# Reordering the first tiles and tile 21 of a fused convolution and quantized feed-forward kernel

## What is computed

```python
out  = conv(x, weight, K=9, groups=4) + einsum('nd,od->no', c, c_weight)[:, :, None] + bias[None, :, None]
fake_quant(t, axis): s = max(max(|t|) / 127, 1e-8); q = clip(round(t / s), -128, 127) * s
qlinear(x, w) = einsum('bsh,oh->bso', fake_quant(x, -1), fake_quant(w, 1))
h    = silu(qlinear(out, w_gate)) * qlinear(out, w_up)      # 1376 wide
x    = x + qlinear(h, w_down)                               # back to 512
```

## Time and profile before

| what | value |
|---|---|
| median of 3 runs | 294.35 us (294.17 to 295.05) |
| profiled execution, its time | 294.47 us |
| profiled execution, its span | 292.9 us |
| busy: TensorE, weight loads | 281.7 us (96%), 164.4 us (56%) |
| busy: VectorE, ScalarE, GpSimd | 251.0, 194.3, 202.0 us (86%, 66%, 69%) |
| granted TensorE clock | full in all 40 slices |
| scale_gate (L803), all forms | 628 ns mean, 96 times |
| multiply_up (L813), all forms | 691 ns mean, 96 times |
| reduction of token_scales (L819) | 1576 ns mean, 32 times |
| scale_silu (L525), all forms | 1163 ns mean, 96 times |
| silu (L635), all forms | 674 ns mean, 96 times |
| round_h (L640), convert_h (L648), all forms | 1414 and 1309 ns mean, 32 times each |
| add_residual (L533) | 1273 ns mean, 24 times |

### The profile page before, as it was taken

How to read it: one execution, slowest core, us unless ns; L and a number is a source line. 1 busy time by engine, 2 the same in 40 slices (tenths; PEclk the granted TensorE clock), 3 DMA queues, 4 the chain that set the end, 5 groups by cost and what they waited for, 6 DMA issues and landing times.

```text
span 292.9 us, 4778 instructions
## 1 busy us (share of the span) xinstructions
PE 281.7 (96%) x1621; PEld 164.4 (56%) x1621; DVE 251.0 (86%) x405; ACT 194.3 (66%) x232; POOL 202.0 (69%) x213
## 2 busy tenths in 40 slices
PE   7998999999999999999999999999989999999995
PEld 7897656655455555554444556665434444444443
DVE  3879879999998988989888878897978889888885
ACT  2258999996686666564888845455688866666640
POOL 1595899998776766663788835556578887666623
PEclk9999999999999999999999999999999999999999
DMA  7999963579846877755489996524256684433355
GB/s 261 416 408 357 410 133 72 113 166 273 214 144 160 203 168 165 208 149 119 128 214 299 239 241 195 166 49 124 73 157 157 159 177 114 87 86 85 100 99 202
DMA packets 83847, 53.36 MB, mean 182 GB/s; under 512 B 69904, under 2 KB 70672, under 8 KB 83696
## 3 DMA queue, kind: packets, MB, share of 16 engines
q1 hardware_dynamic: 83536, 52.89, 67.3%
q10 hardware_dynamic: 288, 0.18, 0.3%
HBM read 27.75 MB, written 8.39 MB: 123 GB/s over the span
## 4 chain that ended last, share of the span: by engine, by line
PE 64%; DVE 9%; POOL 9%; DMA 7%; ACT 5%; issue 4%; SPq 1%; DVEq 0%; POOLq 0%
PE bank L1047 38%; PE bank L1067 19%; PE bank L931 7%; POOL sg_mem L525 4%; DMA xq_mem<-yq_mem 3%; DMA slab<-x_windows 3%; DVE h_mem L813 2%; DVE h_max L819 2%; POOL xq_mem L499 1%; DVE y_part L745 1%; DMA hq_mem<-hq_mem 1%; DVE sg_mem L803 1%; DVE gu_max L704 1%; POOL y_mem L499 1%; ACT sg_mem L635 1%
## 5 line engine op out<-in xcount | busy, mean ns | idle before, releaser
L1047 PE MATMUL bank<-wgu_t,xq_mem 128*128 128x512 bf16 (+1 forms) x768 | 155.9, 357 | 3.1 <-DVE h_mem L813 2.0
L525 POOL TENSOR_TENSOR sg_mem<-sg_mem,gu_scale_row 128x512 f32<-128x512 f32 (+1 forms) x96 | 111.4, 1163 | 64.3 <-ACT sg_mem L635 64.0
L1047 PEld LDWEIGHTS bank<-wgu_t,xq_mem 128*128 128x128 bf16 x768 | 73.7, 98 | 75.2 <-DVE h_mem L813 8.8
L635 ACT ACTIVATE sg_mem<-sg_mem,x_scale 128x512 f32<-128x512 f32 (+1 forms) x96 | 63.7, 674 | 42.5 <-DVE sg_mem L803 42.1
L1067 PE MATMUL bank<-wd_t,hq_mem 128*128 128x512 bf16 (+1 forms) x341 | 78.6, 379 | 0.5 <-DMA hq_mem<-hq_mem 0.5
L813 DVE SCALAR_TENSOR_TENSOR h_mem<-bank,x_scale,sg_mem 128x512 f32<-128x512 f32 (+1 forms) x96 | 66.2, 691 | 10.3 <-POOL sg_mem L525 9.1
L803 DVE TENSOR_TENSOR sg_mem<-bank,gu_scale_row 128x512 f32<-128x512 f32 (+1 forms) x96 | 60.3, 628 | 16.0 <-PE bank L1047 15.6
L640 ACT ACTIVATE h_mem<-h_mem,h_inv 128x1376 f32<-128x1376 f32 (+1 forms) x32 | 45.3, 1414 | 28.1 <-DVE h_inv L697 28.0
L1067 PEld LDWEIGHTS bank<-wd_t,hq_mem 128*128 128x128 bf16 (+1 forms) x341 | 33.3, 98 | 40.9 <-DMA hq_mem<-hq_mem 1.0
L819 DVE TENSOR_REDUCE h_max<-h_mem 128x1 f32<-128x1376 f32 x32 | 50.4, 1576 | 0.0
L931 PE MATMUL bank<-toeplitz_cut,slab 128*128 128x160 f32 (+1 forms) x320 | 44.6, 290 | 1.9 <-DMA slab<-x_windows 1.7
(11 more groups left out here) (63 smaller groups left out, 138.4 us busy)
## 6 DMA issues: line engine op xcount, KB each, us to landing
slab<-x_windows SPq DMA_DIRECT2D x32, 320.0 KB, 5.4
xo_mem<-x SPq DMA_DIRECT2D x24, 256.0 KB, 3.0
out<-xo_mem SPq DMA_DIRECT2D x24, 256.0 KB, 2.2
hq_mem<-w_gate_up SPq DMA_DIRECT2D x6, 512.0 KB, 6.8
slab<-w_down SPq DMA_DIRECT2D x3, 688.0 KB, 12.5
h_mem<-w_gate_up SPq DMA_DIRECT2D x4, 512.0 KB, 13.6
slab<-x SPq DMA_DIRECT2D x1, 2048.0 KB, 9.3
out<-slab SPq DMA_DIRECT2D x7, 256.0 KB, 2.0
```

The costliest lines, as they stand in the source:

```text
L525: pool.tensor_tensor(s, s, gu_scale_row[:, 1, at:at + n], ALU.mult).then_inc(silu_scaled, 1)
L635: act.activation(s, s, ACT.Silu, scale=x_scale[:, i:i + 1]).then_inc(silu_done, 1)
L1047: last = pe.matmul(bank[n % 2][:, 0:cols], xq_t[:, g, k, P * c:P * (c + 1)], wgu_t[:, m, k, at:at + cols], start=(k == 0), stop=(k == KT - 1))
```

## The change

It touches all five engines' lists in the front, and the loops at tiles 0, 1 and 21. TensorE: gate product (0,0) goes ahead of turn_gate_up(7), and turn_xq(6) ahead of gate product (0,2). VectorE: weight tiles 8 and 9 get a scale and an inverse each in place of one pair for both, tile 10's scale comes from GpSimd to VectorE, right behind its maximum, multiply_up(0,0) goes ahead of weights_down(0) and (1), and multiply_up(1,0) ahead of token_scales(0). GpSimd: scale_silu(0,0) goes ahead of round_w(10), and scale_silu(1,0) ahead of the conversion of channels 2 and 3. ScalarE: copy_xq(3) goes ahead of copy_gate_up(7), copy_xq(4) ahead of silu(0,0), copy_xq(6) ahead of round_down(0), copy_span(9) behind it, silu(1,0) ahead of round_y(2) and (3); at tile 21 convert_h(20) goes ahead of the rounding of channels 24 and 25. SP's list is the same.

```diff
--- before.py
+++ after.py
@@ -246,7 +246,7 @@
                    ("scales", 2, 0), ("scales", 2, 1)]
         XQ_BANKS = [gate_bank[0], gate_bank[1], gate_bank[0], gate_bank[1], up_bank[1], down_bank[1], down_bank[0]]
         W_LATE = 6
-        SCALED_BY_POOL = (2, 4, 6, JT - 1)
+        SCALED_BY_POOL = (2, 4, 6)
         BY_PE = 2
 
         def use(kind, part, m):
@@ -283,7 +283,8 @@
         FOLDS_AT.update({i: [q for q in at if q % 2] for i, at in SPANS_AT.items() if at[0] >= 2 * SPANS + 2 and at[-1] % 2})
         FOLDS_AT[7] = [2 * SPANS + 1]
         FOLDS_AT.pop(20)
-        FOLDS_AT[21] = [SLOTS - 1]
+        GROUP_3_AT = 21
+        FOLDS_AT[GROUP_3_AT] = [SLOTS - 1]
 
         def down_bank_of(i):
             return conv_bank(i) if TILES - 3 <= i < TILES - 1 else down_bank[i % 2]
@@ -513,8 +514,6 @@
             scale_w(6, 1)
             for j in range(6, JT - 1):
                 round_w(j)
-            scale_w(JT - 1, 1)
-            round_w(JT - 1)
 
             def scale_silu(i, p):
                 at, n = PIECES[p]
@@ -532,8 +531,11 @@
                 pool.wait_ge(down_scaled, i + 1)
                 pool.tensor_tensor(xo_of(i), xo_of(i), down_out[:, i % 2, :], ALU.add).then_inc(out_ready, 1)
 
+            scale_silu(0, 0)
+            round_w(JT - 1)
             for i in range(TILES):
-                scale_silu(i, 0)
+                if i > 1:
+                    scale_silu(i, 0)
                 if i >= LAG + 1:
                     add_residual(i - LAG - 1)
                 scale_silu(i, 1)
@@ -548,6 +550,8 @@
                 for n in EARLY_CHANNELS_AT.get(i, []):
                     convert_y(n)
                 scale_silu(i, 2)
+                if i == 0:
+                    scale_silu(1, 0)
                 for n in CHANNELS_AT.get(i, []):
                     convert_y(n)
                 for q in SHIFTS_AT.get(i, []):
@@ -625,8 +629,8 @@
             copy_xq(2)
             copy_gate_up(5)
             copy_gate_up(6)
+            copy_xq(3)
             copy_gate_up(7)
-            copy_xq(3)
 
             def silu(i, p):
                 at, n = PIECES[p]
@@ -648,21 +652,22 @@
                 act.activation(hq[i % HQ_BUFS][:, first:INTER], h[i % H_BUFS][:, first:], ACT.Copy, bias=-MAGIC)\
                     .then_inc(hq_ready, 1)
 
+            copy_xq(4)
             silu(0, 0)
-            copy_xq(4)
             copy_span(8)
             copy_gate_up(8)
             silu(0, 1)
             copy_gate_up(9)
-            copy_span(9)
             copy_gate_up(10)
             copy_xq(5)
+            copy_xq(6)
             for o in down_at(-1):
                 round_down(o)
-            copy_xq(6)
+            copy_span(9)
             for i in range(TILES):
+                if i > 1:
+                    silu(i, 0)
                 if i:
-                    silu(i, 0)
                     silu(i, 1)
                 if i == DOWN_ROW_AT + 1:
                     copy_down_row()
@@ -676,12 +681,16 @@
                     round_y(n)
                 if i < TILES - 1:
                     silu(i, 2)
+                if i == 0:
+                    silu(1, 0)
+                if i == GROUP_3_AT:
+                    convert_h(i - 1)
                 for n in CHANNELS_AT.get(i, []):
                     round_y(n)
                 for q in SPANS_AT.get(i, []):
                     if q in BY_ACT:
                         copy_span(q)
-                if i:
+                if i and i != GROUP_3_AT:
                     convert_h(i - 1)
             round_h(TILES - 1)
             convert_h(TILES - 1)
@@ -788,9 +797,11 @@
             weights_scale(7, 1)
             weights_inverse(7, 1)
             weights_top(8)
+            weights_scale(8, 1)
+            weights_inverse(8, 1)
             weights_top(9)
-            weights_scale(8, 2)
-            weights_inverse(8, 2)
+            weights_scale(9, 1)
+            weights_inverse(9, 1)
 
             def scale_gate(i, p):
                 at, n = PIECES[p]
@@ -845,11 +856,15 @@
                     multiply_up(i - 1, 2)
                 else:
                     weights_top(JT - 1)
+                    weights_scale(JT - 1, 1)
+                    weights_inverse(JT - 1, 1)
                 scale_gate(i, 1)
                 if i == 0:
-                    weights_inverse(JT - 1, 1)
+                    multiply_up(i, 0)
                 if i == TILES - 1:
                     scale_gate(i, 2)
+                if i == 1:
+                    multiply_up(i, 0)
                 if i:
                     token_scales(i - 1)
                 else:
@@ -859,7 +874,8 @@
                 if i == 0:
                     for o in down_at(0):
                         weights_down(o)
-                multiply_up(i, 0)
+                if i > 1:
+                    multiply_up(i, 0)
                 if i == 0:
                     multiply_up(i, 1)
                 if LAG < i < TILES - 1:
@@ -1022,7 +1038,6 @@
             conv_span(9)
             turn_gate_up(6)
             turn_xq(3)
-            turn_gate_up(7)
 
             def gate_or_up(i, m, p):
                 bank, done, free = ((gate_bank, gate_done, gate_scaled), (up_bank, up_done, h_ready))[m]
@@ -1075,6 +1090,7 @@
                     pe.wait_ge(yq_turned[i % YQ_BUFS], 16 * ((i - BY_PE) // YQ_BUFS + 1))
                 gate_or_up(i, 0, 0)
                 if i == 0:
+                    turn_gate_up(7)
                     turn_xq(4)
                     gate_or_up(i, 1, 0)
                 gate_or_up(i, 0, 1)
@@ -1087,15 +1103,14 @@
                     conv_span(10)
                     turn_gate_up(10)
                     turn_xq(5)
+                    turn_xq(6)
                 if LAG < i < TILES - 1:
                     down(i - LAG)
                 if i:
                     for q in SPANS_AT.get(i, []):
                         conv_span(q)
                 gate_or_up(i, 0, 2)
-                if i == 0:
-                    turn_xq(6)
-                else:
+                if i:
                     gate_or_up(i, 1, 1)
                 if i in (LAG, TILES - 1):
                     down(i - LAG)
```

## The result

The changed kernel takes 294.52 us (median of 20 runs, 294.08 to 296.29), the kernel before, run beside it, 293.77 us (median of 20, 293.69 to 295.05). The ratio is 1.0036 with a 95% interval of 1.0026 to 1.0046: slower by 0.36%, where the forecast was 0.4% faster. Its single times fall into groups: 12 of 20 take 294.08 to 294.69, one 295.32, and 7 take 295.81 to 296.29. The mean granted clock of TensorE tells them apart: 0.992 to 0.994 in those seven, 0.998 to 1.000 in the other thirteen.

A forecast was written before the change was run, and what follows sets the result against it. TensorE, busy 96% of the span, was taken as the bound, with gains only at its stops. From the profiled 294.47, +0.15 for the front and −1.24 at tile 21 gave 293.38, 293.2 at the median; range 292.0 to 294.7.

The forecast's parts named there:

- Tile 21: At tile 21, convert_h(20) fills ScalarE's wait and the stop at up(22,2) goes: net gain 1.24 us, bounds 0 and 1.3.
- 0.47 + 0.39 = 0.86 us of VectorE: Front, VectorE: one more scale and inverse pair, and tile 10's pair exposed, add 0.86 us.
- the forecast's bounds of −2.1 and +1.1: Whole front, taken as +0.15 us: −2.1 if three stops' removal all counts, +1.1 if ScalarE's delay and landing cost.
- The end of the gain at turn_xq(6) and round_down(0): Tile 0: ScalarE must sit through copy_xq(6), so round_down(0) starts at 36.68 against 36.51 and the gain stops.
- That early lead is worth nothing: Tile 1: TensorE reaches up(1,2) at 43.1, not 44.46, but meets up product (2,0) again, ending 51.64 for 51.60.
- With the w_down transposes over a microsecond further ahead I take 2.4: 44.8: Ahead of gate(2,0): token transposes issued at 42.3 land 2.4 us later, at 44.8, instead of taking 3.3.
- The forecast's own rule, a tenth for each tenth after 45.1: Token transposes of tile 2: each tenth of landing after 45.1 costs a tenth; 4.9 us at a 7.7 landing.
- rival (c): Before gate(2,0): channel 2's transposes, issued later, land late; up to 298.0 us, stop of over 3 us; chance 0.05.
- rival (b): Front costs more, round_h(0) and landing at upper bounds: 294.2 us, tile 6 starting after 76.3; chance 0.25.
- so no part of it is about clock: Whole kernel: granted clock is at its upper level, 2.4 GHz, in every slice, so clock gets no term.
- Channel 2's issue: SP's queue: the first token transposes of tile 2 are issued at 42.3, not 41.18.
- ScalarE behind token_scales(0): Tile 1: round_h(0) waits for token_scales(0), 44.47 for 43.85, +0.62; by silu(2,1) only +0.15 remains.

The follow-up runs named there:

- e1: Kernel before with only tile 21's edit, convert_h(20) ahead of the rounding of channels 24 and 25: ratio 0.9953 to the kernel before, median 292.78 us.
- e7: Changed kernel with all of tile 1's part undone, tiles 0 and 21 as changed: ratio 0.9972 to the kernel before, 293.27 us.
- e13: The changed kernel again, unaltered, one more profiled execution: 294.29 us, beside one run of the kernel before at 294.30.
- e9: Changed kernel plus one TensorE wait ahead of up(1,2) for the maximum of token_scales(0): ratio 0.9975 to the kernel before, 293.27 us.
- e4: Changed kernel with token_scales(0) ahead of multiply_up(1,0) on VectorE again: ratio 0.9976 to the kernel before.
- e2: Changed kernel with the old order at tile 21, so the front's edits alone: ratio 1.0108 to the kernel before, 297.82 us.
- e12: Kernel before with tile 21's part and gate(0,0) ahead of weight tile 7, copies to match, VectorE's list unchanged: ratio 0.9950 to the kernel before.
- e6: Changed kernel with round_w(10) ahead of scale_silu(0,0) on GpSimd again: ratio 1.0113 to the kernel before.
- e5: Changed kernel with weight tile 10's scale on GpSimd again, ahead of scale_silu(0,0), its inverse behind scale_gate(0,1): ratio 1.0074 to the kernel before.
- e3: Changed kernel with channels 2 and 3 rounded and converted ahead of silu(1,0) and its multiply: ratio 1.0019 to the kernel before.

## Why the prediction was wrong, step by step

**Tile 21: right.** Forecast: convert_h(20) into the wait, silu(22,0) 1.24 earlier, the up product (22,0) directly behind token_scales(21), no stop at up(22,2), net 1.24 us. ScalarE and VectorE of the kernel after, against the earlier trace rows:

```profile
209.51 1.33 ACT L652 ACTIVATE hq_mem<-h_mem 128x1376 bf16<-128x1376 f32 x1
211.66 1.34 ACT L584 ACTIVATE y_mem<-y_mem,x_inv 128x512 f32<-128x512 f32 x2 [0.82 <-DVE x_inv L706]
212.90 1.32 ACT L639 ACTIVATE sg_mem<-sg_mem,x_scale 128x512 f32<-128x512 f32 x2
```

```profile
215.00 0.16 DVE L706 RECIPROCAL h_inv<-h_scale 128x1 f32<-128x1 f32 x1
215.11 0.75 DVE L824 SCALAR_TENSOR_TENSOR h_mem<-bank,x_scale,sg_mem 128x512 f32<-128x512 f32 x1
```

The absolute times are some 2.2 us later than forecast, which is the front's loss in this execution; relative to each other they stand as forecast. GpSimd's multiply (22,0), at 213.69, waits for nothing that is late (the earlier trace rows had it idle 1.24). `e1` measures 1.4 us for it. The 0.14 forecast at up(23,0) did not show, and the small stop that the forecast saw there in the kernel before isn't in its timeline either, which has one block from 214.96 on the earlier trace rows.

**VectorE in the front: one term mis-sized.** "0.47 + 0.39 = 0.86 us of VectorE" took tile 10's pair at 0.39; its scale alone took 1.04, because it was held until GpSimd's multiply had ended. The scales of tiles 8 and 9 took 0.33 each, held in the same way, so 0.45 with the inverse until the next instruction starts, close to the 0.47 taken. The forecast costed a VectorE instruction by its own row and looked only at what it waits for, not at what runs beside it. It is a term of some 0.7 us on VectorE, and it pushed tile 10's rounding to 33.67 for the 32.9 forecast. What all of tile 0's part cost in the end, by `e7` less `e1`, is 0.55 us, not clear of its noise (0.46 by the length of the front, `e7` less before, from one profile each), within the forecast's bounds of −2.1 and +1.1.

**The end of the gain at turn_xq(6) and round_down(0): right in kind.** The forecast said that ScalarE must sit through copy_xq(6) and so passes on nothing to tile 1. In the profile after round_down(0) starts at 37.51; of this, 0.34 is a later start of this execution (convolution span 9 at 25.88 for 25.54), the rest tile 10's scale.

**"That early lead is worth nothing": the step that failed, together with the landing.** The forecast had TensorE at up(1,2) at 43.1 without its stop, and "With the w_down transposes over a microsecond further ahead I take 2.4: 44.8". The reason given for 2.4 holds: the three profiles with such a gap and no packet under way have 2.3. What was missing is that the fetch of TensorE's next 16 KB of instructions moves with TensorE's own progress. In the profiles with the changed order on TensorE and its number of warm-up matmuls, all but `e7` (1.5 us), the packet came within some 0.7 us of the end of tile 1's products, wherever that end lay (44.5 to 46.3). With the stop at up(1,2) gone the fetch came at 44.5 and fell upon the transposes. The landing moved from the forecast 44.8 to 47.7 in the profile after and to 46.7 in `e13`. The forecast's own rule, a tenth for each tenth after 45.1, gives 2.6 and 1.6 us for these; the change less `e7` is 1.25 us by the medians (294.52 less 293.27) and 1.9 by the ratios (0.64% of 294), of the same size, and by the length of the front 1.1 (`e13`) and 1.8 us (the profile after). So rival (c) happened, at a chance of 0.05, by a cause that it did not name: it looked at how full SP's queue was, which it rightly called light. Its sign, a stop of over 3 us, was not met (2.83 and 2.14); that of rival (b) was, as tile 6 starts at about 77.9 (75.78 and 12 matmuls).

**"... so no part of it is about clock": a term put at nothing.** The forecast gave TensorE's clock no term, as it was full in every slice before. The stop that the change made brought one. The seven executions with a mean granted clock of 0.992 to 0.994 took 296.06 us on average, the thirteen others 294.35: 1.7 us more in 7 of 20, or 0.6 us of tile 1's 1.9. None of the 24 executions of `e7` and `e9`, which have no such stop, is below 0.998.

**What taking the lead away does.** The lead was not worth nothing but did harm: `e9` takes it away by a wait and gains 0.6%, and `e4` likewise.

**Channel 2's issue.** Forecast 42.3, found 43.23 and 42.89. Of the 0.9, tile 10's scale has most and the later start of the profiled execution the rest.

**ScalarE behind token_scales(0).** The forecast had round_h(0) wait, "44.47 for 43.85", +0.62. Found: 45.38, with an idle time of 0.63 before it.

```profile
43.39 1.58 DVE L830 TENSOR_REDUCE h_max<-h_mem 128x1 f32<-128x1376 f32 x1
...
45.38 1.44 ACT L644 ACTIVATE h_mem<-h_mem,h_inv 128x1376 f32<-128x1376 f32 x1 [0.63 <-DVE h_inv L706]
```

The rule was right, and its time carries the 0.9 of the term above. It had no consequence of its own, since the transposes came later still.

**The sum.** Forecast: +0.15 in the front, −1.24 at tile 21. Measured by parts, each a difference of two ratios times 294 us: tile 21 −1.4 (`e1`), tile 0 +0.55 (`e7` less `e1`), tile 1 +1.9 (the change less `e7`), together +1.05 us. They add up by construction, so the sum proves nothing. Tile 21's and tile 1's parts are clear of noise, tile 0's is not.

**`e2` against the change.** By its ratio `e2` stands 0.72% above the change, where tile 21's part is worth 0.47. The clock accounts for it: five of its six executions have the low mean clock, and seven of the change's twenty. Among these alone the means of 297.91 and 296.06 us, each over the mean of the kernel before beside it (294.41 and 293.94), are 0.47% apart.

**A faster version.** `e1` (0.9953) and `e12` (0.9950) beat both kernels. What is to be kept of the change is convert_h(20) in the wait for the group's inverse.

**What stays open.** Why the packet comes at 48.0 in the kernel before and at 45.5 in `e1`, whose TensorE list is the same. What makes the landing 3.8 in one execution and 4.5 in the next. How the packet delays a transpose (no run held a transfer engine free of it). And why the clock falls behind the stop in some executions of the change and not in others.

## What to carry to other kernels

An engine that is given a lead does more than wait at the next wait: here its instruction fetches moved too, and one of 16 KB took the landing of a transfer for which it had to wait from 2.3 to as much as 4.5 us. Before a stop is removed just ahead of a transfer that is due, look at what the transfer queues do in that half microsecond, the instruction queue among them. Where a change can bring a stop of over 2 us on TensorE, give the clock a term too, even if it was full before: here it cost 1.7 us more in 7 of 20 executions. And when a small VectorE operation is put somewhere new, price it by what GpSimd does beside it, not by its own row from another place; filling a wait with work that is ready, as at tile 21, paid in full here.

## What the runs showed of the hardware that was not expected

**Small VectorE instructions held by GpSimd.** A scale of 96 x 2 elements took 0.17 us with GpSimd idle (`e6`) and 1.04 beside a multiply of 128 x 512, ending with it. The Trainium skill ("SBUF — State Buffer", Who interferes with whom) has a port pair that the two engines share under an exclusive lock, and the rows agree for this form. They don't show it for every form: in `e5` a reciprocal of the same size ran beside the same multiply and took 0.15.

```profile
32.53 0.15 DVE L727 RECIPROCAL gu_inv<-gu_scale 96x2 f32<-96x2 f32 x1
```

**Instruction packets among transposes.** For the first transpose of a pair 3.8 to 4.5 us to landing with one, 2.3 to 3.3 without, for the second 3.0 to 4.8 and 2.4 to 2.6, in 13 profiles (table above). Where the packet met the first, SP's issue of the two also took longer, 3.13 to 3.94 us instead of 2.50 to 2.56.

**A stop can cost a second time, by the clock.** In `e5` TensorE stood still for 2.54 us before gate(2,0), and the 12 matmuls behind took 4.28 instead of 2.76. Its timeline, and busy time by stretch (PE, PEld, DVE, ACT, POOL, granted clock, DMA share, GB/s):

```profile
47.09 4.28 PE L1062 MATMUL bank<-wgu_t,xq_mem 128*128 128x512 bf16 x12 [2.54 <-DMA xq_mem<-yq_mem]
```

```profile
46.00:48.00 2.00, 0.91 (x3) 0.36 (x4) 1.93 (x4) 2.00 (x4) 0.94 (x2) 0.70 0.21 13
48.00:50.00 2.00, 2.00 (x6) 0.68 (x5) 1.02 (x3) 1.62 (x3) 1.71 (x3) 0.50 0.00 0
50.00:52.00 2.00, 2.00 (x13) 1.42 (x12) 1.65 (x3) 1.19 (x3) 1.27 (x1) 0.95 0.78 177
```

A granted clock of 0.50 is the lower level, 1.2 GHz, and it cost 4.28 − 2.76 = 1.52 us. The same happened in `e6` after two stops of 2.5 us, but not in the profile after, whose stop was longer (2.83), nor in the profiles of `e2` and `e13` (2.14). The mean clock of single executions says that it is no rarity: it is 0.992 to 0.994 in 7 of 20 of the change, 5 of 6 of `e2`, 3 of 4 of `e5` and 4 of 4 of `e6`, and never that low in the 63 executions of `e1`, `e3`, `e4`, `e7`, `e9` and `e12`.
